# Splitting the modulation-weight loads of an AdaLN block over three DMA-issuing engines

## The chip, the cores and the metric

One Trainium2 chip, all 8 of its cores. Each core runs the same program on its own share of the tokens, with no exchange between cores. The metric is the device time of the slowest core in microseconds (us).

## The reference

One AdaLN transformer block on x of 4 x 4096 x 1024 in f32: six modulation vectors from a small condition c, attention between two layer norms, and a feed-forward layer whose operands are quantized to FP4 in blocks of 16. Cut to what the change touches and what uses it:

```python
mod = (silu(c) @ wmod).reshape(4, 6, 1, 1024)          # c: 4 x 1024, wmod: 1024 x 6144, f32
sa, ca, ga, sb, cb, gb = (mod[:, i] for i in range(6))
ga = (2 * (ga >= 0) - 1) * maximum(abs(ga), 0.25)      # gb likewise
h = layernorm(x) * (1 + ca) + sa
x = x + ga * attention(h, w_qkv, w_proj, b_proj)       # 16 heads
h = layernorm(x) * (1 + cb) + sb
x = x + gb * ffn_fp4(h, w_gate, w_up, w_down)          # 1024 -> 2816 -> 1024
```

## The kernel before

Two cores share one of the four sequences. A core owns 2048 tokens (its queries and its output) and computes keys and values for all 4096. x is kept channel-major, as `x_own`, 128 partitions x 8 x 2048 in f32 (8 MB). The program is a row of stages, each closed by `barrier()`, at which every engine waits for all semaphores: p0 (the modulation vectors), p1 (layer norm and the projections to q and k in slices of 512 tokens), pv (v), p3 (attention, with the quantization of the weights beside it on VectorE), p35 and p4 (softmax sums and output projection), p5 (second layer norm and quantization), p6 (feed-forward).

The change lies in p0. There the order on each engine is the order in which the code calls `em`, `dma` and `wt`:

- SP issues four loads at once: `ident32`, `ccol` (the condition), `bpcol` (a bias) and `x_own` in one transfer of 8 MB.
- ScalarE waits for `ccol` and `bpcol` and computes `silu_c` (L253).
- `wmod`, 1024 x 6144 f32, comes in KC = 8 chunks of 128 rows, 3 MB each, into two buffers `wmod_buf[kc % 2]`. All eight are issued by GpSimd (POOL). From the third on, GpSimd first waits until TensorE has finished the chunk that was in the buffer (`wm_done`).
- TensorE waits for the chunk (`t_wm`), for kc = 0 also for `silu_c`, and runs 48 matmuls on it, each of them a 128 x 128 block of `wmod` as stationary operand against one column of `silu_c` (L263). All 8 x 48 = 384 products add up in `mod_ps`. (The profile counts two instructions for each of these f32 matmuls, 768 in all.)
- VectorE copies `mod_ps` to `modc` (L272), makes `ca1`, `cb1`, `gacol` and `gbcol` from it, and the barrier follows. Then SP issues the loads of `xo` and GpSimd those of `wqk`, and p1 begins.

A DMA is issued through `_q_issue`. Each issuing engine has four semaphores that it takes in turn, and it waits for the transfer four places earlier in its own list before it issues the next:

```python
            s = QSEMS[q][QIDX[q]]
            QIDX[q] = (QIDX[q] + 1) % NQSEM
            wt(q, s, s.v)
            em(q, fn, s, 16)
```

Transfers issued by GpSimd run in the profile's queue q0 (software_dynamic), those issued by SP in q1 (hardware_dynamic). ScalarE issues none in the kernel before.

Of the kernel before, what the change touches and what calls it, by code (L numbers as in the profile page):

```python
# [14 lines left out]
P = 128  # L15
# [3 lines left out]
def build(cfg):  # L19
    N, D, NH, FI, SL = cfg["N"], cfg["D"], cfg["NH"], cfg["FI"], cfg["SL"]  # L20
# [24 lines left out]
    wmod_in = nc.dram_tensor("wmod", [D, 6 * D], F32, kind="ExternalInput").ap()  # L45
# [23 lines left out]
    def sb(name, shape, dt, stack=None):  # L69
        return (stack or es).enter_context(nc.sbuf_tensor(name, shape, dt))  # L70

    def psum(name, parts, free, dt=F32, stack=None):
        esz = 4 if dt == F32 else 2
        banks = -(-free * esz // 2048)
        return (stack or es).enter_context(
            nc.psum_tensor(name, [parts, banks * 2048 // esz], dt))
# [9 lines left out]
    mP, mV, mA = Sem("mP"), Sem("mV"), Sem("mA")  # L86
# [21 lines left out]
    with nc.Block("mk") as blk:  # L108
# [3 lines left out]
        def em(eng, fn, inc=None, k=1):  # L112
            if inc is None:
                E[eng](fn)
                return None
            inc.v += k
            E[eng](lambda e, fn=fn, h=inc.h, k=k: fn(e).then_inc(h, k))
            return inc.v

        def _q_issue(q, fn):  # L120
# [4 lines that stand above are left out]
            return (s, s.v)  # L125

        def dma(q, dst, src):
            return _q_issue(q, lambda e, dst=dst, src=src: e.dma_start(dst, src))
# [4 lines left out]
        def wtt(eng, tok):  # L133
            if tok:
                wt(eng, tok[0], tok[1])
# [5 lines left out]
        def wt(eng, sem, v=None):  # L141
            v = sem.v if v is None else v
            E[eng](lambda e, h=sem.h, v=v: e.wait_ge(h, v))

        def dr(eng):
            E[eng](lambda e: e.drain())  # L146

        def barrier():
            for eng in ("sync", "gpsimd", "scalar", "vector", "tensor"):
                for s in ALL_SEMS:  # L150
                    wt(eng, s)

        def act_table(set_id):
            E["scalar"](lambda e, i=set_id: e.add_instruction(  # L154
                mybir.InstLoadActFuncSet(
                    name=nc.get_next_instruction_name(),
                    act_func_set_id=i, ins=[], outs=[])))
# [76 lines left out]
        with contextlib.ExitStack() as p0:  # L234
            silu_c = sb("silu_c", [P, KC], F32, p0)
            wmod_buf = [sb(f"wmod{i}", [P, 6 * D], F32, p0) for i in range(2)]
            mod_ps = psum("mod_ps", P, 6 * KC, F32, p0)

            act_table(18)
            em("vector", lambda e: e.memset(ones128[:], 1.0))  # L240
            em("vector", lambda e: e.memset(ones1x[:], 1.0))
            em("vector", lambda e: e.memset(eps5[:], 1e-5), mV)
            em("vector", lambda e: e.memset(eps30[:], 1e-30), mV)
            t_id = dma("sync", ident32[:], ident_in[:])
            t_cc = dma("sync", ccol[:], cvec_in[:])
            t_bp = dma("sync", bpcol[:], bproj_in[:])
            dma("sync", x_own[:], xr[:, :, 0:T])
            wtt("vector", t_id)
            em("vector", lambda e: e.tensor_copy(identbf[:], ident32[:]), mV)
            dr("vector")  # L250
            wtt("scalar", t_cc)
            wtt("scalar", t_bp)
            v_silu = em("scalar", lambda e: e.activation(silu_c[:], ccol[:], AF.Silu), mA)  # L253
            wm_done = [0, 0]
            for kc in range(KC):
                if kc >= 2:
                    wt("gpsimd", mP, wm_done[kc % 2])
                t_wm = dma("gpsimd", wmod_buf[kc % 2][:], wmod_in[P * kc:P * (kc + 1), :])
                wtt("tensor", t_wm)
                if kc == 0:  # L260
                    wt("tensor", mA, v_silu)
                for m in range(6 * KC):
                    em("tensor", lambda e, kc=kc, m=m: e.matmul(  # L263
                        mod_ps[:, m:m + 1],
                        wmod_buf[kc % 2][:, P * m:P * (m + 1)],
                        silu_c[:, kc:kc + 1],
                        start=(kc == 0 and m == 0),
                        stop=(kc == KC - 1 and m == 6 * KC - 1)),
                        mP if m == 6 * KC - 1 else None)
                wm_done[kc % 2] = mP.v  # L270
            wt("vector", mP, mP.v)
            em("vector", lambda e: e.tensor_copy(modc[:], mod_ps[:, 0:6 * KC]), mV)  # L272
            dr("vector")
            cam = modc[:, 1 * KC:2 * KC]
            gam = modc[:, 2 * KC:3 * KC]
            cbm = modc[:, 4 * KC:5 * KC]
            gbm = modc[:, 5 * KC:6 * KC]
            em("vector", lambda e: e.tensor_scalar(ca1[:], cam, 1.0, None, ALU.add))
            em("vector", lambda e: e.tensor_scalar(cb1[:], cbm, 1.0, None, ALU.add))
            dr("vector")  # L280
            for g_src, g_dst in ((gam, gacol), (gbm, gbcol)):
                em("vector", lambda e, s=g_src, d=g_dst: e.scalar_tensor_tensor(
                    d[:], s, -1.0, s, ALU.mult, ALU.max))
                em("vector", lambda e, s=g_src: e.tensor_scalar(
                    smallf[:, 0:KC], s, 0.0, 2.0, ALU.is_ge, ALU.mult))
                dr("vector")
                em("vector", lambda e: e.tensor_scalar(
                    smallf[:, 0:KC], smallf[:, 0:KC], -1.0, None, ALU.add))
                em("vector", lambda e, d=g_dst: e.tensor_scalar(
                    d[:], d[:], 0.25, None, ALU.max))  # L290
                dr("vector")
                em("vector", lambda e, d=g_dst: e.tensor_tensor(
                    d[:], d[:], smallf[:, 0:KC], ALU.mult), mV)
                dr("vector")
            barrier()
# [822 lines left out]
def _get_nc():  # L1118
    if "nc" not in _NC_CACHE:
        _NC_CACHE["nc"] = build(CFG)  # L1120
    return _NC_CACHE["nc"]
# [44 lines left out]
if __name__ == "__main__":  # L1166
    nc = build(CFG)
    n = sum(1 for _ in nc.all_instructions())
    print("built OK; instructions:", n)
```

How the kernel before makes its waits and increments, by code:

```python
        def em(eng, fn, inc=None, k=1):  # L112
            if inc is None:
                E[eng](fn)
                return None
            inc.v += k
            E[eng](lambda e, fn=fn, h=inc.h, k=k: fn(e).then_inc(h, k))
            return inc.v
# [22 lines left out]
        def wt(eng, sem, v=None):  # L141
            v = sem.v if v is None else v
            E[eng](lambda e, h=sem.h, v=v: e.wait_ge(h, v))
```

## Time and profile before

| | us |
|---|---|
| median of the two timed runs (4413.93 and 4420.41) | 4417.17 |
| the profiled execution, device time | 4420.6 |
| its span on the slowest core, core 0 | 4419.1 |
| spans of the eight cores | 4396.6 to 4419.1 |
| TensorE busy (matmul) | 2298.0 |
| VectorE busy | 2800.1 |
| ScalarE busy | 1193.3 |
| GpSimd busy | 201.9 |

The profile is of core 0. Its span counts from the first to the last instruction, and the device time of that execution is 1.5 us more. Shares over the whole span mix eight stages, so for a change in one stage the time of that stage is to be looked at: p0 is the first 184 us or so, 4% of the span.

### The profile page before, as it was taken

What the parts mean: (1) busy time and instruction counts of PE and PEld (TensorE: products, weight loads), DVE (VectorE), ACT (ScalarE), POOL (GpSimd) and SP (SyncE); (2) the same over time, 40 slices, a digit from 0 to 9 for tenths busy, and PEclk for the clock granted to TensorE, in tenths of its full rate; (3) what the DMA queues carried; (4) which work ended last, traced back from release to release, by engine and by line L of the source; (5) the groups of instructions that cost most, each with busy time, mean ns of one, the idle gap of its engine ahead of it and who ended that gap; (6) DMA issues with size and microseconds to landing.
All of it is one profiled execution on the core that took longest, in us unless ns stands there. A gap on an engine that the chain in (4) does not pass through costs nothing.

```text
span 4419.1 us, 32886 instructions; the slowest of 8 cores (4396.6 to 4419.1 us)
## 1 busy us (share of the span) xinstructions
PE 2298.0 (52%) x9132; PEld 858.5 (19%) x9132; DVE 2800.1 (63%) x4084; ACT 1193.3 (27%) x1236; POOL 201.9 (5%) x324
## 2 busy tenths in 40 slices
PE   8656654978787878756555600022222164222227
PEld 8612211422222222211100200001111121111113
DVE  0066665329999999999712569966666724666661
ACT  0011111088898989866500000000000000000000
POOL 0001100000111010010000000000000000000000
PEclk9987877989999989977755755556666577666658
DMA  7511112312222222232310010011111012111102
GB/s 248 124 45 36 49 60 92 72 40 57 72 72 72 53 71 69 61 78 58 85 39 15 25 37 14 14 29 29 29 29 29 20 49 69 29 29 29 29 24 86
DMA packets 260929, 239.47 MB, mean 54 GB/s; under 512 B 193040, under 2 KB 229264, under 8 KB 256656
## 3 DMA queue, kind: packets, MB, share of 16 engines
q1 hardware_dynamic: 233360, 122.27, 10.9%
q0 software_dynamic: 27392, 115.11, 8.8%
q8 instruction: 79, 1.29, 0.1%
q14 instruction: 98, 0.80, 0.1%
HBM read 157.36 MB, written 46.66 MB: 46 GB/s over the span
## 4 chain that ended last, share of the span: by engine, by line
DVE 42%; PE 21%; DVEq 14%; DMA 10%; issue 5%; ACT 5%; SPq 3%; POOL 0%; ACTq 0%; POOLq 0%
DVEq L232 7%; DVEq L222 4%; PE dp_ps L1085 4%; ACT pb L738 3%; PE mod_ps L263 3%; PE bc L802 3%; PE v_ps L582 2%; SPq L131 2%; DVEq L146 2%; DMA wu_sb<-wuts 2%; PE g_ps L1034 2%; PE u_ps L1044 2%; DVE x_own L211 2%; DVE x_own L213 2%; DVE x_own L209 2%
## 5 line engine op out<-in xcount | busy, mean ns | idle before, releaser
L738 ACT ACTIVATE pb<-s_ps,negc 128x1024 bf16<-128x1024 f32 x1024 | 1037.0, 1233 | 118.3 <-PE s_ps L710 117.6
L1034 PE MATMUL g_ps<-wg_sb,h2q 128*128 128x512 bf16 (+1 forms) x768 | 189.4, 406 | 1282.0 <-DMA wu_sb<-wuts 1233.2
L706 PE MATMUL s_ps<-qb,kb 64*128 64x512 bf16 x1024 | 394.2, 388 | 183.3 <-ACT pb L738 116.3
L721 PE MATMUL pv_ps<-pb,vres 128*65 128x512 bf16 x992 | 414.5, 418 | 87.4 <-DVE O L772 87.4
L710 PE MATMUL s_ps<-qb,kb 64*128 64x512 bf16 x1024 | 407.1, 400 | 0.0
L1052 ACT ACTIVATE silu_sb<-g_ps 128x1024 bf16<-128x1024 f32 (+1 forms) x56 | 47.1, 840 | 1280.3 <-PE u_ps L1044 1280.3
L727 PE MATMUL pv_ps<-pb,vres 128*65 128x512 bf16 x992 | 389.6, 393 | 0.0
L1034 PEld LDWEIGHTS g_ps<-wg_sb,h2q 128*128 128x128 bf16 x768 | 81.9, 108 | 1383.3 <-issue 1317.3
L1057 DVE TENSOR_TENSOR hmul<-silu_sb,u_ps 128x1024 bf16<-128x1024 bf16 (+1 forms) x56 | 55.6, 992 | 430.6 <-ACT silu_sb L1052 356.2
L154 ACT ACT_TABLE_LOAD x5 | 6.4, 1283 | 933.6 <-DVE x_own L849 311.4
L464 PE MATMUL qk_ps<-h,wqk 128*128 128x512 bf16 x768 | 211.5, 426 | 34.5 <-ACT qkst L476 19.6
L706 PEld LDWEIGHTS s_ps<-qb,kb 64*128 64x128 bf16 x1024 | 94.0, 93 | 656.4 <-issue 656.4
L1085 PE MATMUL dp_ps<-hq,wd 128*128 128x512 bf16 x704 | 162.1, 395 | 73.6 <-DMA wd<-wdts 59.4
L802 PE MATMUL bc<-lnsums,ones1x 1*64 1x512 f32 x128 | 123.8, 1068 | 137.4 <-DMA lnsums<-lnsums 91.9
L263 PE MATMUL mod_ps<-silu_c,wmod 128*128 128x1 f32 x768 | 164.1, 352 | 16.6 <-ACT silu_c L253 16.0
L721 PEld LDWEIGHTS pv_ps<-pb,vres 128*65 128x65 bf16 x992 | 108.4, 109 | 325.7 <-issue 325.7
L263 PEld LDWEIGHTS mod_ps<-silu_c,wmod 128*128 128x128 f32 x768 | 164.0, 333 | 16.6 <-issue 16.6
L1044 PE MATMUL u_ps<-wu_sb,h2q 128*128 128x512 bf16 (+1 forms) x768 | 166.5, 370 | 0.0
L807 DVE TENSOR_TENSOR O<-O,bc 64x512 bf16<-64x512 bf16 x64 | 43.9, 685 | 186.6 <-PE bc L802 186.6
L476 ACT CAST qkst<-qk_ps 128x512 bf16<-128x512 f32 x96 | 56.2, 585 | 345.8 <-DVE qkn L440 306.4
L1097 DVE SCALAR_TENSOR_TENSOR x_own<-dp_ps,gbcol,x_own 128x512 f32<-128x512 f32 x32 | 24.0, 750 | 176.5 <-PE dp_ps L1085 173.5
L440 DVE TENSOR_REDUCE qkn<-nrm_ps 1x1 f32<-1x512 f32 x192 | 122.0, 671 | 12.3 <-PE nrm_ps L430 10.7
(170 smaller groups left out, 3824.2 us busy)
## 6 DMA issues: line engine op xcount, KB each, us to landing
wmod<-wmod POOLq DMA_DIRECT2D x8, 3072.0 KB, 13.2
x_own<-x SPq DMA_DIRECT2D x2, 8192.0 KB, 44.7
x_own<-wgate POOLq DMA_DIRECT2D x22, 512.0 KB, 4.6
x_own<-wup POOLq DMA_DIRECT2D x22, 512.0 KB, 4.6
x_own<-wdown POOLq DMA_DIRECT2D x16, 704.0 KB, 5.9
wd<-wdts SPq DMA_DIRECT2D x88, 128.0 KB, 2.1
wg_sb<-wgts SPq DMA_DIRECT2D x10, 1024.0 KB, 5.6
wu_sb<-wuts SPq DMA_DIRECT2D x10, 1024.0 KB, 8.0
```

The source lines that it names most:

```text
L232: V(lambda e: e.drain())
L263: em("tensor", lambda e, kc=kc, m=m: e.matmul(mod_ps[:, m:m + 1], wmod_buf[kc % 2][:, P * m:P * (m + 1)], silu_c[:, kc:kc + 1], start=(kc ...
L464: em("tensor", lambda e, oc=oc, kc=kc, pb=pb, bi=bi: e.matmul(qk_ps[pb][:, 0:SL], wqk_sb[kc][:, P * oc:P * (oc + 1)], h_buf[bi][:, kc, :], ...
L706: em("tensor", lambda e, kt=kt, qoff=qoff, pb=pb, sAB=sAB: e.matmul(sAB[:, 0:512], kbuf[pb][0:64, P * kt:P * (kt + 1)], qbuf[pb][0:64, qof ...
L710: em("tensor", lambda e, kt=kt, qoff=qoff, pb=pb, sAB=sAB: e.matmul(sAB[:, 512:1024], kbuf[pb][64:128, P * kt:P * (kt + 1)], qbuf[pb][64:1 ...
L721: em("tensor", lambda e, ktp=ktp, qs2p=qs2p, gp=gp, h0=h0: e.matmul(pv_ps[0][:, 512 * qs2p:512 * (qs2p + 1)], vres[:, ktp, 65 * h0:65 * (h ...
L727: lambda e, ktp=ktp, qs2p=qs2p, gp=gp, h1=h1: e.matmul(pv_ps[1][:, 512 * qs2p:512 * (qs2p + 1)], vres[:, ktp, 65 * h1:65 * (h1 + 1)], pbuf ...
L738: exp_at[g] = em("scalar", lambda e, sAB=sAB, pAB=pAB: e.activation(pAB[:, 0:1024], sAB[:, 0:1024], AF.Exp, bias=negc[:], scale=0.125), mA)
L802: p_bc = em("tensor", lambda e, qs=qs, b_=b_: e.matmul(bc_ps[b_:b_ + 64, 0:512], ones1x[:, 0:64], lnsums[0:1, QS * qs:QS * (qs + 1)], star ...
L1034: em("tensor", lambda e, kc=kc, qt=qt, iw=iw, tb=tb, tbase=tbase, off=off: e.matmul(g_ps[tb][:, off:off + iw], h2q[:, kc, tbase + P * qt:t ...
L1044: p_gu = em("tensor", lambda e, kc=kc, qt=qt, iw=iw, tb=tb, tbase=tbase, off=off: e.matmul(u_ps[tb][:, off:off + iw], h2q[:, kc, tbase + P ...
L1085: lambda e, ic=ic, ib=ib, j=j, qs=qs: e.matmul(dp_ps[2 * j + qs][:, 0:512], wd_sb[ib][:, P * j:P * (j + 1)], hq[:, ic, 512 * qs:512 * (qs ...
```

## The change

Every 3 MB chunk of `wmod` is loaded by two transfers of 1.5 MB, columns 0 to 3071 and columns 3072 to 6143. The two are issued by two different engines, which are taken in turn from the list GpSimd, SP, ScalarE: chunk kc has its left half from engine kc mod 3 and its right half from engine (kc + 1) mod 3. Both engines wait for the buffer from kc = 2 on, and TensorE waits for both halves before its 48 matmuls. Nothing else is edited.

| chunk | left half | right half |
|---|---|---|
| 0, 3, 6 | GpSimd | SP |
| 1, 4, 7 | SP | ScalarE |
| 2, 5 | ScalarE | GpSimd |

```diff
             wm_done = [0, 0]
+            wm_qs = ["gpsimd", "sync", "scalar"]
             for kc in range(KC):
                 if kc >= 2:
-                    wt("gpsimd", mP, wm_done[kc % 2])
-                t_wm = dma("gpsimd", wmod_buf[kc % 2][:], wmod_in[P * kc:P * (kc + 1), :])
+                    wt(wm_qs[kc % 3], mP, wm_done[kc % 2])
+                    wt(wm_qs[(kc + 1) % 3], mP, wm_done[kc % 2])
+                t_w1 = dma(wm_qs[kc % 3], wmod_buf[kc % 2][:, 0:3 * D],
+                           wmod_in[P * kc:P * (kc + 1), 0:3 * D])
+                t_wm = dma(wm_qs[(kc + 1) % 3], wmod_buf[kc % 2][:, 3 * D:6 * D],
+                           wmod_in[P * kc:P * (kc + 1), 3 * D:6 * D])
+                wtt("tensor", t_w1)
                 wtt("tensor", t_wm)
```

On SP, in p0, the new loads stand behind that of `x_own` (`d_sync0` to `d_sync3` are SP's four semaphores, `mP` is TensorE's; `wmod0` and `wmod1` are the two buffers):

```order
 L128 DMA x_own<-x 128x8x2048
+L143 UNCONDITIONAL_BRANCH
+L117 UNCONDITIONAL_BRANCH [waits d_sync0]
+L128 DMA wmod0<-wmod 128x3072
+L143 UNCONDITIONAL_BRANCH
+L117 UNCONDITIONAL_BRANCH [waits d_sync1]
+L128 DMA wmod1<-wmod 128x3072
+L143 UNCONDITIONAL_BRANCH
+L143 UNCONDITIONAL_BRANCH [waits mP]
+L117 UNCONDITIONAL_BRANCH [waits d_sync2]
+L128 DMA wmod1<-wmod 128x3072
```

The right half of chunk 0 is thus SP's fifth transfer and the left half of chunk 1 its sixth, and neither waits for a matmul.

On ScalarE, in p0, the first load stands behind the activation that makes `silu_c`:

```order
 L253 ACTIVATE silu_c<-ccol 128x8
+L143 UNCONDITIONAL_BRANCH
+L117 UNCONDITIONAL_BRANCH [waits d_scalar0]
+L128 DMA wmod1<-wmod 128x3072
+L143 UNCONDITIONAL_BRANCH
+L143 UNCONDITIONAL_BRANCH [waits mP]
+L117 UNCONDITIONAL_BRANCH [waits d_scalar1]
+L128 DMA wmod0<-wmod 128x3072
```

ScalarE now issues five transfers in this stage, where it issued none, and the first of them is the right half of chunk 1.

On GpSimd, in p0, five transfers of half a chunk stand where eight of a whole one stood. The first rows of the kernel before:

```order
L117 UNCONDITIONAL_BRANCH [waits d_gpsimd0]
L128 DMA wmod0<-wmod 128x6144
L143 UNCONDITIONAL_BRANCH
L117 UNCONDITIONAL_BRANCH [waits d_gpsimd1]
L128 DMA wmod1<-wmod 128x6144
```

and of the kernel with the change:

```order
L117 UNCONDITIONAL_BRANCH [waits d_gpsimd0]
L128 DMA wmod0<-wmod 128x3072
L143 UNCONDITIONAL_BRANCH
L143 UNCONDITIONAL_BRANCH [waits mP]
L117 UNCONDITIONAL_BRANCH [waits d_gpsimd1]
L128 DMA wmod0<-wmod 128x3072
```

GpSimd's second transfer now waits for a matmul: it is the right half of chunk 2.

## Rows read from the trace of the kernel before

**Rows 1.** The timeline of p0: start us, us, engine line op, idle before

```profile
2.56 0.39 SPq L128 DMA_DIRECT2D x_own<-x  x1
...
15.65 0.21 ACT L253 ACTIVATE silu_c<-ccol 128x8 f32<-128x8 f32 x1 [13.31 <-DMA bpcol<-bproj]
...
16.00 41.09 PE L263 MATMUL mod_ps<-silu_c,wmod 128*128 128x1 f32 x192 [16.00 <-ACT silu_c L253]
37.23 0.53 POOL L128 DMA_DIRECT2D wmod<-wmod  x1 [34.35 <-PE mod_ps L263]
...
57.67 123.01 PE L263 MATMUL mod_ps<-silu_c,wmod 128*128 128x1 f32 x576 [0.57 <-DMA wmod<-wmod]
57.72 0.53 POOL L128 DMA_DIRECT2D wmod<-wmod  x1 [19.95 <-PE mod_ps L263]
...
180.79 0.21 DVE L272 COPY modc<-mod_ps 128x48 f32<-128x48 f32 x1 [177.52 <-PE mod_ps L263]
...
183.91 1.00 SPq L128 DMA_DIRECT2D xo<-x  x2
```

**Rows 2.** Landing times of wmod's eight loads; then of its first two alone

```profile
DMA to landing us min/median/max: 12.0/13.2/26.1
...
DMA to landing us min/median/max: 13.7/19.9/26.1
```

**Rows 3.** DMA issues of the whole page: KB each, median us to landing

```profile
x_own<-x SPq DMA_DIRECT2D x2, 8192.0 KB, 44.7
...
wg_sb<-wgts SPq DMA_DIRECT2D x10, 1024.0 KB, 5.6
wu_sb<-wuts SPq DMA_DIRECT2D x10, 1024.0 KB, 8.0
```

**Rows 4.** DMA issues of the first 190 us, the same columns

```profile
x_own<-x SPq DMA_DIRECT2D x1, 8192.0 KB, 58.3
xo<-x SPq DMA_DIRECT2D x2, 2048.0 KB, 31.4
...
ident<-ident SPq DMA_DIRECT2D x1, 64.0 KB, 1.8
...
bpcol<-bproj SPq DMA_DIRECT2D x1, 4.0 KB, 13.5
```

**Rows 5.** DMA of the first 15 us: packets and queues

```profile
DMA packets 588, 3.59 MB, mean 239 GB/s; under 512 B 317, under 2 KB 445, under 8 KB 445
...
q0 software_dynamic: 158, 3.51, 79.2%
q1 hardware_dynamic: 430, 0.07, 2.5%
```

**Rows 6.** Stretches: us, busy of PE, PEld, DVE, ACT, POOL, PEclk, DMA share, GB/s

```profile
0.00:8.00 8.00, 0.00 (x0) 0.00 (x0) 0.46 (x5) 1.28 (x1) 1.42 (x6) 1.00 0.70 190
0.00:14.00 14.00, 0.00 (x0) 0.00 (x0) 0.46 (x5) 1.28 (x1) 1.42 (x6) 1.00 0.81 233
...
28.00:37.00 9.00, 9.00 (x44) 9.00 (x43) 0.00 (x0) 0.00 (x0) 0.00 (x0) 1.00 1.00 343
37.00:57.00 20.00, 20.00 (x95) 20.00 (x94) 0.00 (x0) 0.00 (x0) 0.53 (x1) 1.00 1.01 333
```

**Rows 7.** DMA moved in the first 39 us, then in the first 44 us

```profile
DMA packets 1363, 11.64 MB, mean 298 GB/s; under 512 B 336, under 2 KB 464, under 8 KB 464
...
DMA packets 1503, 13.15 MB, mean 299 GB/s; under 512 B 336, under 2 KB 464, under 8 KB 464
```

**Rows 8.** Landing times of the loads of xo in the first barrier's wake

```profile
DMA to landing us min/median/max: 20.5/31.4/42.2
```

**Rows 9.** Spans and clocks of the cores

```profile
core 0: 4419.1 us, clock 0.753
...
core 3: 4396.6 us, clock 0.752
```

## The prediction

> **What bounds the kernel now.** The change touches only the first stage, so I read the timeline of that stage first, to see what each matmul of the modulation product waited for. TensorE starts at 16.00 us and runs to 57.09 (192 instructions), waits 0.57 us, and runs from 57.67 to 180.68 (576 instructions) [rows 1]. That is 768 instructions in 164.1 us, 0.2137 us each, 20.5 us for a chunk of 96, in one row without a gap but for those 0.57 us. The granted clock is 1.00 in all stretches of it, the upper level, also before TensorE had begun [rows 6]. So from 16 us on the stage is bound by TensorE, and the loads are hidden under it: a chunk of 3 MB lands 12.0 to 26.1 us after its issue, 13.2 in the middle [rows 2], and has a chunk's 20.5 us for it.
>
> What decides the start is the second thing to see. TensorE waited for `silu_c`, that for `bpcol` [rows 1], which took 13.5 us to land while `ident`, issued 1 us earlier in the same queue, took 1.8 [rows 4]. The view of the queues shows why: in the first 15 us the software queue moved 3.51 MB, which is chunk 0 and a little of chunk 1, and the hardware queue 0.07 MB, the three small loads [rows 5]. `x_own` had moved nothing. It was issued at 2.56 and landed 58.3 us later, at 60.9 [rows 1, 4], and nobody in this stage wants it. Chunk 0, issued ahead of it at 1.67 us, landed 13.7 us later, at 15.4 [rows 2]. The kernel before thus has its order of urgency right, because the urgent data are in another queue than the bulky ones.
>
> The DMA engines themselves are full: 343 GB/s in 28 to 37 us, where only `x_own` was under way, and 333 in 37 to 57, where chunk 2 was beside it [rows 6]. A second queue adds no bandwidth.
>
> **The change part by part.** *The matmuls.* The same 768, in the same order, 164.1 us. No gain from loads that are faster, since only 0.57 us of waiting for a load is there.
>
> *The right half of chunk 0.* This is the term that counts. It is issued by SP right behind `x_own`, without any wait. Are transfers of one hardware queue served one after the other or side by side? The trace has two pairs issued back to back on SP. `wg_sb` and `wu_sb`, 1 MB each, land after 5.6 and 8.0 us [rows 3]; at 343 GB/s 1.05 MB takes 3.1 us, so the second lands one such time behind the first, less the half microsecond by which it was issued later. The two `xo` loads land after 20.5 and 42.2 us [rows 8], the second twice as late. Both pairs look like one after the other; side by side the two of a pair would land together. So chunk 0 is whole only when `x_own` is through. Sizes: the left half of chunk 0, 1.57 MB; `x_own`, 8.39; the right half of chunk 0, 1.57; the small loads, 0.07. That is 11.6 MB. ScalarE issues the right half of chunk 1 (1.57 MB) once `silu_c` is done, near 10 us, in a queue of its own. Is that ahead of the end or behind it? The trace has no transfer issued by ScalarE. Ahead of it, the sum is 13.2 MB, behind it 11.6. In the kernel before the later software transfer got its share beside `x_own` (chunk 2 landed within 20 us in the middle of it [rows 1]), so I take 13.2.
>
> When has this core moved so much? The trace of before says so directly, as the DMA engines were full there too from about 3 us on: 11.64 MB by 39 us and 13.15 MB by 44.0 [rows 7]. So 13.2 MB by 44.1. From the last byte to the release of the waiting engine add 1.5 us: chunk 0 (3.15 MB) was through at about 14 us (233 GB/s x 14 us = 3.26 MB [rows 6]) and landed at 15.4. TensorE starts at 45.6 us where it started at 16.0: 29.6 us later. With 11.6 MB it is 39 + 1.5 = 40.5, 24.5 us later, the lower bound if the queue is in order. For the upper one I take the slowest rate of a large transfer in that queue: two loads of `x_own` have the median 44.7, the first took 58.3, so the reload in the middle of the kernel took 31.1 us [rows 3, 4], 270 GB/s. The left half is through at 8 us (190 GB/s x 8 = 1.52 MB [rows 6]), the other 11.6 MB take 43.0: start at 51.0, 35 us later.
>
> The Trainium skill (page DMA: Bandwidth & Descriptors, section Queues, rings and completion order) says that SP and ScalarE each own one ring on each of the same 16 DMA engines, that descriptors of a ring are taken in order, and that an engine goes round between the rings that have work. By that rule the ScalarE half gets its turns beside `x_own`, and the sum is 13.2 MB. No row here shows the ScalarE ring.
>
> *`silu_c`.* With only 1.57 MB ahead of it in the software queue, `bpcol` should land near 8 us and not at 15.6. That is worth 7 us only if chunk 0 were there, and it isn't. Nothing gained.
>
> *Chunk 1.* Its left half is the next in SP's queue, 1.57 MB behind chunk 0: 4.6 us at 343 GB/s, landing at about 50. Chunk 0's matmuls last until 45.6 + 20.5 = 66.1, so it is covered by 16 us.
>
> *Chunks 2 to 7.* Both halves are issued when the buffer is free, and have 20.5 us. At that time nothing else is under way, unlike in the kernel before, where chunk 2 had `x_own` beside it: issued at 37.23, landed at 57.67, the 0.57 us of waiting [rows 1]. That wait goes: -0.6. The 16 transfers of half a size in place of 8 cost issue time on SP, ScalarE and GpSimd (about 0.5 us each [rows 1]), which do nothing else in this stage. In the four-place rotation the transfer waited for is always one of earlier chunks or, for the left half of chunk 4 on SP, `x_own`, long landed by then. If that cover were gone, each late chunk would cost its excess over 20.5 us; that is a rival below.
>
> *The rest.* VectorE's small work and the barrier (180.68 to 183.9) move as they are. The loads of `xo` and `wqk` are issued after the barrier with all slots free, as before. `x_own` lands at about 42 us in place of 60.9, which is of use to nobody before 184. Later stages have the same instructions.
>
> Sum: +29.6 - 0.6 = +29.0 us, with bounds +24 and +34. The profiled execution took 4420.6, 3.4 us above the median of the runs shown (4417.2). So a profiled run like it would be 4450, and against the median I predict 4446 us, 0.7% slower. A comparison of this kernel can tell about 2% (88 us) from no change, so this is "within 2%".
>
> The same page of the Trainium skill (section Rules for kernel authors) says that spreading DMAs over SP, ACT and GpSimd for bandwidth doesn't help, as all run on the same 16 engines. The trace agrees: 333 GB/s with both queues, 343 with one [rows 6]. A gain from the split alone would be 0 by the rule and 0.57 us by the row.
>
> **The rivals.** *Transfers of one queue run side by side.* Then the right half of chunk 0 doesn't wait for all of `x_own`. If it comes with the left one, chunk 0 is whole at 15.4 as before and TensorE starts there: -0.6 - 0.6, 4416. If four transfers share 343 GB/s evenly from 8 us on (`x_own`, this half, two of chunk 1), it takes 6.28 MB, 18 us, and with 1.5 us TensorE starts at 27.8: +11, 4428. In the best case the start follows the earlier `silu_c`, at about 8.5: 4409. For it: `ident` and `ccol` landed quickly though more was issued behind them, which proves little. Against it: both pairs of rows 3 and 8. Chance 0.09.
>
> *The hardware queue carries less than in the stretch I read.* In my sum the rate before 28 us is partly the software queue's. At 270 GB/s it gives +34.4: 4452. For it: the reload's 31.1 us. Against it: 343 GB/s at 28 to 37 us in that same queue. Chance 0.09.
>
> *Slower by much: the later chunks become late.* Two halves on two queues, one of them served after the other, and TensorE waits for the later one. The place is the wait at the head of each chunk, the price seven times the excess over 20.5 us. If every chunk took 26.1 us, as the slowest did [rows 2], it would be 7 x 5.6 = 39, in all +68: 4485. At the 42.2 us of the slowest `xo` load it would be 7 x 21.7 = 152, in all +181: 4598. It passes 2% from 20.5 + (88 - 29) / 7 = 28.9 us a chunk. Against it: both of those rows had 5 MB or more beside them; 3.15 MB at 333 GB/s takes 9.4 us and the latency 1.5. Chance 0.03, of which 0.02 above 2%.
>
> **How the numbers follow.** The in-order case (forecast) has 0.79, the three rivals 0.09, 0.09 and 0.03. The range goes from 4428 (the even sharing) to 4462: the upper bound 4452 and 10 us for what one execution differs from another, as the cores of one run already lie 4396.6 to 4419.1 apart [rows 9]; about 0.15 lies outside. Faster by over 2% needs 88 us out of a stage with 0.57 us of waiting for loads and 16 us of start: 0.01. Slower by over 2% is the third rival's part: 0.02. Within 2%: 0.97.
>
> **What would show it.** Right: no matmul of the first product before 40 us, released by a `wmod` load; `silu_c` done near 9 us; `x_own` landing near 42 us, the right half of chunk 0 some 5 us later; then 164 us of matmuls without a gap; `xo` issued at about 213 us and not 183.9; the later stages as long as before. Wrong: TensorE starting before 30 us (side by side), a wait before chunk 2 or later (late chunks), or a difference that arises after the first barrier.

## The result and the profile after

The changed kernel took 4470.35 us (median of 23 runs, 4445.48 to 4509.45), the kernel before 4420.0 (median of 22 runs, 4412.63 to 4461.3). The ratio is 1.0092, with a 95% interval of 1.0063 to 1.012; it and the medians differ because it leaves out runs in which a die had a clearly lower clock, and as the profiled run of the changed kernel has a little of that on its second die (0.731 against 0.752), I read it on core 0, which has the clock of before. The interval is 28 to 53 us, 41 in the middle: slower by less than the 2% that count as a difference. The forecast was +29 us, 4446, within 4428 to 4462; 1.0092 x 4417.2 is 4458.

The timeline of the first stage on core 0 of the changed kernel (start us, us, what, idle before) answers to [rows 1]:

```profile
1.68 0.69 POOL L128 DMA_DIRECT2D wmod<-wmod  x1 [0.98 <-POOLq L38]
2.10 0.38 SPq L128 DMA_DIRECT2D bpcol<-bproj  x1
2.56 0.39 SPq L128 DMA_DIRECT2D x_own<-x  x1
3.06 170.57 SPq L128 DMA_DIRECT2D wmod<-wmod  x6
...
12.57 0.21 ACT L253 ACTIVATE silu_c<-ccol 128x8 f32<-128x8 f32 x1 [10.22 <-DMA bpcol<-bproj]
12.64 161.03 ACTq L128 DMA_DIRECT2D wmod<-wmod  x5
...
50.16 163.97 PE L269 MATMUL mod_ps<-silu_c,wmod 128*128 128x1 f32 x768 [50.16 <-DMA wmod<-wmod]
71.43 0.54 POOL L128 DMA_DIRECT2D wmod<-wmod  x1 [69.07 <-PE mod_ps L269]
...
214.24 0.21 DVE L278 COPY modc<-mod_ps 128x48 f32<-128x48 f32 x1 [210.91 <-PE mod_ps L269]
...
217.36 1.00 SPq L128 DMA_DIRECT2D xo<-x  x2
```

TensorE starts at 50.16 us where it started at 16.00, and what released it is no longer `silu_c` (done at 12.8) but a load of `wmod`. Then all 768 instructions run in one row of 163.97 us: the 0.57 us of before is gone. The loads of `xo`, the first thing behind the barrier, are issued at 217.36 in place of 183.91, 33.5 us later; over the eight cores this shift is 33.5 to 36.9 us. The lowest runs of the two kernels stand as far apart, 32.9 us (4445.48 and 4412.63). Of the two profiled executions, the whole spans of cores 1 to 3 differ by about as much (29.5, 35.5 and 32.7 us), that of core 0 by only 17.7: behind the first stage core 0 of the kernel before took 15.8 us longer than core 0 of the changed one, cores 1 to 3 between 1.6 us less and 5.4 us more. So the loss is read from the first stage, not from core 0's span.

The DMA issues of the first 50 us on the same core (KB each, us to landing) show the order in SP's ring:

```profile
x_own<-x SPq DMA_DIRECT2D x1, 8192.0 KB, 43.7
wmod<-wmod SPq DMA_DIRECT2D x2, 1536.0 KB, 47.6
wmod<-wmod POOLq DMA_DIRECT2D x1, 1536.0 KB, 10.6
wmod<-wmod ACTq DMA_DIRECT2D x1, 1536.0 KB, 14.8
```

`x_own` lands at 2.56 + 43.7 = 46.3 us. The 47.6 is the median of SP's two halves, 46.9 and 48.3. The half of chunk 0 behind `x_own` lands at 3.06 + 46.9 = 50.0, when its sibling from GpSimd has been there since 12.3. ScalarE's half of chunk 1, issued at 12.64, is there at 27.4: it got its turns beside `x_own`. The Trainium skill (DMA: Bandwidth & Descriptors, section Queues, rings and completion order) says that SP and ScalarE own one ring each on every DMA engine and that the engine goes round between them; the 14.8 us of that row agree, and the queue view now lists ScalarE's transfers by themselves, as q10.

### The profile page after: what moved, and what is told of

Its sections match the earlier page's. It is cut to its first block, busy times and chain, and to the rows that moved or that the text cites. A ratio compares the mean times of both kernels' runs of the same rounds, so it can differ in the third digit from the quotient of the medians.

```text
span 4468.3 us, 32837 instructions; the slowest of 8 cores (4429.3 to 4468.3 us)
## 1 busy us (share of the span) xinstructions
PE 2338.9 (52%) x9053; PEld 865.6 (19%) x9132; DVE 2801.4 (63%) x4084; ACT 1195.8 (27%) x1236; POOL 200.4 (4%) x321
## 3 DMA queue, kind: packets, MB, share of 16 engines
q10 hardware_dynamic: 720, 7.86, 0.6%
## 4 chain that ended last, share of the span: by engine, by line
DVE 39%; PE 22%; DVEq 13%; DMA 10%; ACT 7%; issue 6%; SPq 3%; POOL 0%; ACTq 0%; POOLq 0%
DVEq L232 7%; ACT pb L744 6%; PE dp_ps L1091 4%; PE mod_ps L269 4%; DVEq L222 4%; PE bc L808 3%; PE v_ps L588 2%; SPq L131 2%; PE g_ps L1040 2%; DVEq L146 2%; DMA wu_sb<-wuts 2%; PE u_ps L1050 2%; PE pj_ps L844 2%; DVE x_own L213 1%; DVE x_own L209 1%
## 5 line engine op out<-in xcount | busy, mean ns | idle before, releaser
L1040 PE MATMUL g_ps<-wg_sb,h2q 128*128 128x512 bf16 (+1 forms) x755 | 199.8, 425 | 1257.5 <-DMA wu_sb<-wuts 1209.5
L712 PE MATMUL s_ps<-qb,kb 64*128 64x512 bf16 x1024 | 405.6, 399 | 177.3 <-ACT pb L744 119.5
L727 PE MATMUL pv_ps<-pb,vres 128*65 128x512 bf16 x992 | 423.7, 427 | 86.7 <-DVE O L778 86.7
L716 PE MATMUL s_ps<-qb,kb 64*128 64x512 bf16 x1024 | 415.7, 409 | 0.0
L733 PE MATMUL pv_ps<-pb,vres 128*65 128x512 bf16 x992 | 399.3, 403 | 0.0
L1050 PE MATMUL u_ps<-wu_sb,h2q 128*128 128x512 bf16 (+1 forms) x756 | 176.7, 388 | 0.8
```

The costliest lines, as they stand in the source:

```text
L712: em("tensor", lambda e, kt=kt, qoff=qoff, pb=pb, sAB=sAB: e.matmul(sAB[:, 0:512], kbuf[pb][0:64, P * kt:P * (kt + 1)], qbuf[pb][0:64, qof ...
L716: em("tensor", lambda e, kt=kt, qoff=qoff, pb=pb, sAB=sAB: e.matmul(sAB[:, 512:1024], kbuf[pb][64:128, P * kt:P * (kt + 1)], qbuf[pb][64:1 ...
L727: em("tensor", lambda e, ktp=ktp, qs2p=qs2p, gp=gp, h0=h0: e.matmul(pv_ps[0][:, 512 * qs2p:512 * (qs2p + 1)], vres[:, ktp, 65 * h0:65 * (h ...
L733: lambda e, ktp=ktp, qs2p=qs2p, gp=gp, h1=h1: e.matmul(pv_ps[1][:, 512 * qs2p:512 * (qs2p + 1)], vres[:, ktp, 65 * h1:65 * (h1 + 1)], pbuf ...
L1040: em("tensor", lambda e, kc=kc, qt=qt, iw=iw, tb=tb, tbase=tbase, off=off: e.matmul(g_ps[tb][:, off:off + iw], h2q[:, kc, tbase + P * qt:t ...
L1050: p_gu = em("tensor", lambda e, kc=kc, qt=qt, iw=iw, tb=tb, tbase=tbase, off=off: e.matmul(u_ps[tb][:, off:off + iw], h2q[:, kc, tbase + P ...
```

## The experiments

The times of a stage are of core 0, from the timeline, unless other cores are named. Seven of the nine runs ask where the loss is, two try a faster version.

### The load of x_own behind the urgent ones

```diff
-            dma("sync", x_own[:], xr[:, :, 0:T])
             wtt("vector", t_id)
 ...
+                if kc == 1:
+                    dma("sync", x_own[:], xr[:, :, 0:T])
                 wtt("tensor", t_w1)
```

> The changed kernel, with the 8 MB load of x_own issued by SP behind its two first loads of wmod (the right half of chunk 0 and the left half of chunk 1) and not ahead of them. Theory (the right half of chunk 0 waits for x_own because it stands behind it in SP's ring): TensorE's first product starts at 14 to 18 us in place of 50.2, the loads of xo are issued at 180 to 185 us in place of 217.4, and the kernel takes about 34 us less than the changed one, that is the time of the kernel before within 5 us. Rival (the split over three engines is slow in itself, or the engines are simply full): the start stays above 30 us.

```profile
2.56 0.86 SPq L128 DMA_DIRECT2D wmod<-wmod  x2
3.50 0.67 SPq L128 DMA_DIRECT2D x_own<-x  x1
...
15.61 163.97 PE L270 MATMUL mod_ps<-silu_c,wmod 128*128 128x1 f32 x768 [15.61 <-DMA wmod<-wmod]
...
182.80 1.00 SPq L128 DMA_DIRECT2D xo<-x  x2
```

(the timeline of core 0). The start is at 15.61, on the eight cores 15.6 to 16.7, and `xo` is issued at 182.80: on core 0 the whole loss is gone, with the split and the three engines still there. On cores 6 and 7 chunk 2 comes 2.2 and 1.3 us late, and `xo` is issued at 185.3 and 184.8, 2.3 and 0.9 us later than in the kernel before. Against the kernel before the ratio is 1.0011 (0.9969 to 1.0053): no difference is seen, though the interval, from 14 us less to 23 more, is too wide to confirm the "within 5 us" by itself. `x_own` lands at 64.9 us, 18.6 later than in the changed kernel, and nobody minds. The loss was one line's place.

### The same bytes, another ring

```diff
-            dma("sync", x_own[:], xr[:, :, 0:T])
+            dma("scalar", x_own[:], xr[:, :, 0:T])
```

> The changed kernel, with the load of x_own issued by ScalarE, as its first transfer, in place of SP. As many bytes are under way as in the changed kernel, but now the right half of chunk 0 is first in SP's ring, and the right half of chunk 1 is behind x_own in ScalarE's. Theory (order inside a ring): TensorE's first product starts at 15 to 28 us; chunk 1 is whole only when x_own is through, near 50 us, so TensorE stands still between chunk 0 and chunk 1 for 2 to 15 us, and the loads of xo are issued at 215 to 220 us with almost the same loss as in the changed kernel. Rival (all transfers under way share the engines and what counts is their bytes, 13 MB, not the ring): the start is at 45 to 52 us and there is no gap behind chunk 0.

```profile
22.20 0.21 ACT L253 ACTIVATE silu_c<-ccol 128x8 f32<-128x8 f32 x1 [19.86 <-DMA bpcol<-bproj]
...
29.79 20.61 PE L269 MATMUL mod_ps<-silu_c,wmod 128*128 128x1 f32 x96 [29.79 <-DMA wmod<-wmod]
...
53.71 143.49 PE L269 MATMUL mod_ps<-silu_c,wmod 128*128 128x1 f32 x672 [3.31 <-DMA wmod<-wmod]
...
200.43 1.01 SPq L128 DMA_DIRECT2D xo<-x  x2
```

(the timeline of core 0). The same transfers are wanted and the same 13 MB or so are under way, but the start is at 29.8 and not at 50.2. That is 1.8 us above my range, and 15 below the rival's. So the order inside the ring is the larger part, while sharing the engines costs too: 29.8 is 14 us later than with `x_own` behind. Chunk 1, whose half now stands behind `x_own`, makes the gap of 3.31 us (2.3 to 6.5 on the eight cores). For the end I had written 215 to 220, which was wrong arithmetic: 53.71 + 143.5 + 3.2 is 200.4.

### Half of x_own ahead

```diff
-            dma("sync", x_own[:], xr[:, :, 0:T])
+            dma("sync", x_own[:, 0:KC // 2, :], xr[:, 0:KC // 2, 0:T])
 ...
+                if kc == 1:
+                    dma("sync", x_own[:, KC // 2:KC, :], xr[:, KC // 2:KC, 0:T])
```

> The changed kernel, with x_own loaded in two transfers of 4 MB, the first ahead of SP's two loads of wmod as now, the second behind them. The dose is halved. Theory (the start is the time at which the bytes ahead in the ring are through): 4.2 MB less at 290 to 320 GB/s, 13 to 14.5 us, so the start is at 36 to 37.5 us in place of 50.2 and the loads of xo are issued at 203 to 205 us. Rival (any x_own load ahead costs the same, for instance by its issue): 50 us. Rival (the ring isn't the cause): below 20 us.

The start is at 34.37 us (34.1 to 35.9 on the eight cores), and `xo` is issued at 201.57. The dose works: nothing of `x_own` ahead gives 15.6, half of it 34.4, all of it 50.2, that is 18.8 us for the first 4.2 MB and 15.8 for the second. The start is 1.6 us below the range I gave, since 4.2 MB took 15.8 us off and not 14.5 at most: 266 GB/s, less than the 290 I had as the slowest. The rate here is 327 GB/s from 14 to 34 us; it is the changed kernel that has a slow stretch ahead of its start, 184 GB/s in 32 to 38 us, of which more below.

### Whole chunks, all on SP

```diff
-                    wt("gpsimd", mP, wm_done[kc % 2])
-                t_wm = dma("gpsimd", wmod_buf[kc % 2][:], wmod_in[P * kc:P * (kc + 1), :])
+                    wt("sync", mP, wm_done[kc % 2])
+                t_wm = dma("sync", wmod_buf[kc % 2][:], wmod_in[P * kc:P * (kc + 1), :])
```

> The kernel before, with the eight whole chunks of wmod issued by SP, behind x_own, in place of GpSimd: no split, and one engine. Theory (the loss is what stands ahead in the ring): 11.6 MB are ahead of chunk 0's end, TensorE starts at 40 to 46 us, and the loads of xo are issued at 207 to 213 us, a loss of 24 to 29 us. Rival (the split in halves or the three engines cost it): no loss, the start at 16 us.

```profile
4.73 0.21 ACT L253 ACTIVATE silu_c<-ccol 128x8 f32<-128x8 f32 x1 [2.38 <-DMA bpcol<-bproj]
45.58 163.97 PE L263 MATMUL mod_ps<-silu_c,wmod 128*128 128x1 f32 x768 [45.58 <-DMA wmod<-wmod]
...
212.77 1.00 SPq L128 DMA_DIRECT2D xo<-x  x2
```

(the timeline of core 0). The kernel before, with no split and no second engine for `wmod`, loses 28.9 us by having them issued on SP behind `x_own`. The start is at 43.8 to 50.3 on the eight cores, above my 46 on four of them, and the loss is 27.4 to 34.0. `silu_c` is ready at 4.9 us, the earliest of all kernels, and it is of no use.

### The split alone

```diff
-            wm_qs = ["gpsimd", "sync", "scalar"]
+            wm_qs = ["gpsimd"] * 3
```

> The changed kernel with both halves of every chunk issued by GpSimd: the split alone, without the other two engines. Theory (the split costs nothing, only the place behind x_own does): TensorE's first product starts at 15 to 17 us, 164 us of products without a gap of over 1.5 us, and the loads of xo are issued at 182 to 186 us, as in the kernel before. Rival (twice as many transfers cost by themselves): over 190 us.

```profile
11.80 0.21 ACT L253 ACTIVATE silu_c<-ccol 128x8 f32<-128x8 f32 x1 [9.45 <-DMA bpcol<-bproj]
...
19.44 41.09 PE L269 MATMUL mod_ps<-silu_c,wmod 128*128 128x1 f32 x192 [19.44 <-DMA wmod<-wmod]
...
64.62 123.01 PE L269 MATMUL mod_ps<-silu_c,wmod 128*128 128x1 f32 x576 [4.10 <-DMA wmod<-wmod]
...
190.86 1.00 SPq L128 DMA_DIRECT2D xo<-x  x2
```

(the timeline of core 0). A miss: the split isn't free when GpSimd issues both halves. `bpcol` lands 3.9 us earlier than in the kernel before (`silu_c` starts at 11.8, where it was 15.65 [rows 1]), TensorE starts 3.4 us later, released by chunk 0, and chunk 2 makes a gap of 4.10 us where it made 0.57. `xo` is issued 7.0 us later. The queues of the first 15 us (packets, MB, share of 16 engines) show where the time went; in the kernel before they had 158 and 3.51, and 430 and 0.07 [rows 5]:

```profile
q0 software_dynamic: 236, 2.70, 65.5%
q1 hardware_dynamic: 515, 0.75, 16.1%
```

A packet of the software queue is half as large as before (11 KB on average in place of 22), and `x_own`, which stands behind `bpcol` in SP's ring, has moved 0.7 MB by 15 us where it had moved nothing. These are bytes that chunk 0 lacks. So the trace shows that `x_own` gets its turns earlier and that chunk 0 pays; that the size of the packets is the reason was not tested by itself. The changed kernel's late start is not this effect: its left half of chunk 0 is there at 12.3 us, 38 us ahead of the right one.

### Another order of the three engines

```diff
-            wm_qs = ["gpsimd", "sync", "scalar"]
+            wm_qs = ["gpsimd", "scalar", "sync"]
```

> The changed kernel with the three engines taken in the order GpSimd, ScalarE, SP, so that SP's first load of wmod is the right half of chunk 1, and chunk 0 has GpSimd and ScalarE. Theory (only what stands behind x_own in SP's ring is late, and a later chunk has one chunk's time of slack for it): chunk 0's right half is issued at 12 to 13 us behind silu_c and lands some 15 us later, so the first product starts at 25 to 30 us; chunk 1 is whole at 48 to 52 us, a gap of 0 to 5 us; the loads of xo are issued at 194 to 199 us, about 20 us ahead of the changed kernel's 217.4. Rival (three rings in use are slow whatever the order): 210 us or more.

The first product starts at 27.09 us, then there is a gap of 8.88 us before chunk 1, and `xo` is issued at 203.28. So the start is as expected, and the gap and the end are longer than I gave: SP's half of chunk 1 is there at 56.6, not at 48 to 52. On cores 3 to 7 the products end 3.6 to 7.0 us later still, and on core 5 `xo` is issued at 210.3, where the rival's range began; what speaks against the rival is the start at 25.9 to 28.1 on all cores. The direction holds: a half behind `x_own` that is wanted one chunk later has 20.5 us of slack, and the loss is 19 us on core 0 in place of 33.5 (19 to 27 on the eight cores in place of 33.5 to 36.9). Merely swapping two names in the list gives 14 us back on core 0, 8 to 16 over the cores.

### Nothing behind chunk 0

```diff
+                if kc == 1:
+                    wtt("sync", t_wm)
+                    wtt("scalar", t_wm)
                 if kc >= 2:
```

> The changed kernel, with both loads of chunk 1 issued only when chunk 0's right half has landed. So nothing stands behind it in SP's ring and ScalarE issues nothing beside it: 11.6 MB are all that is under way. In the changed kernel the start was at 50.2 us on core 0, 4.6 us behind the 45.6 of my sum. Theory A (the 16 engines don't keep pace, so that part of what stands behind in the ring, and ScalarE's 1.57 MB, are moved before chunk 0 is whole): the start is at 40 to 43 us, as my lower bound for 11.6 MB had it (40.5). Theory B (SP's ring, with x_own alone in it, runs slower than the mixed traffic of the kernel before that I took the curve from): the start is at 44 to 47 us. In both, chunk 1 is whole some 10 to 12 us later, inside chunk 0's 20.5 us of products, without a gap.

The stretches of core 0 (us, busy of PE, PEld, DVE, ACT, POOL, PEclk, DMA share, GB/s), then what had been moved by 40 and by 44 us:

```profile
14.00:28.00 14.00, 0.00 (x0) 0.00 (x0) 0.00 (x0) 0.00 (x0) 0.00 (x0) 1.00 1.00 339
28.00:32.00 4.00, 0.00 (x0) 0.00 (x0) 0.00 (x0) 0.00 (x0) 0.00 (x0) 1.00 1.13 166
...
28.00:36.00 8.00, 0.00 (x0) 0.00 (x0) 0.00 (x0) 0.00 (x0) 0.00 (x0) 1.00 1.02 240
36.00:44.00 8.00, 0.00 (x0) 0.00 (x0) 0.00 (x0) 0.00 (x0) 0.00 (x0) 1.00 0.51 214
```

```profile
DMA packets 1715, 11.22 MB, mean 280 GB/s; under 512 B 339, under 2 KB 467, under 8 KB 467
...
DMA packets 1760, 11.61 MB, mean 264 GB/s; under 512 B 352, under 2 KB 480, under 8 KB 480
```

The start is at 44.28 us (44.1 to 48.4 on the eight cores): theory B's range but for the slowest core, and not for its reason. Of the 11.61 MB only 0.4 were left at 40 us, and they took 4 us more with the engines busy for 0.51 of 36 to 44 us. So the 16 engines don't finish together, and the transfer is whole when the last has finished. The rate is the other part, but SP's ring with `x_own` alone in it isn't slow as such: it moves 339 GB/s from 14 to 28 us, as much as the kernel before. What is missing is missing in 28 to 32 us, 166 GB/s with the engines busy all the time, and the other seven cores fall as well, each to between 119 and 201 GB/s for at least 2 us between 28 and 32 us.

### A version that is faster than both

In the kernel before TensorE stands from the first barrier to 225 us for the loads of `wqk`, though the statistics of the first slice need only `x_own`, which is there. The wait is put where `wqk` is first used. The rows of the kernel before (core 0; the profile puts this wait down to `xo`, on core 6 to `wqk`):

```profile
225.17 0.58 PE L356 MATMUL st_ps<-xbch,ones 128*1 128x512 bf16 x1 [44.49 <-DMA xo<-x]
...
257.10 3.15 PE L464 MATMUL qk_ps<-h,wqk 128*128 128x512 bf16 x7 [13.88 <-DVE h L409]
```

And the edit:

```diff
-            for tok in wqk_toks:
-                wtt("tensor", tok)
 ...
             v_h_cur = emit_h(0)
+            for tok in wqk_toks:
+                wtt("tensor", tok)
```

> The kernel before, with TensorE's wait for the loads of wqk moved from the head of the second stage to behind the statistics and the broadcast of the first slice, which need x_own alone. In the kernel before, TensorE stands from 184 to 225 us for them, and the first projection starts at 257.1. Theory (the same kind of loss as in the change, work that waits for bytes it doesn't need): the first projection starts when wqk is there, at 225 to 230 us, and the kernel takes 25 to 32 us less than before. Rival (the time comes back later, because the next slice or the GpSimd queue is the bound there): the first projection starts earlier, but the end of the second stage moves by less than 10 us.

```profile
198.46 2.04 PE L387 MATMUL bc_ps<-rs_row,ones1x 1*128 1x512 f32 x2 [5.44 <-DVE nmr_row L378]
...
224.09 7.16 PE L462 MATMUL qk_ps<-h,wqk 128*128 128x512 bf16 x23 [21.89 <-DMA hscr<-h]
```

(the timeline of core 0; the releaser named there is `hscr`, but on the other seven cores the same wait is put down to `wqk`, and it is the one that was moved). The first projection starts at 224.1 in place of 257.1, and the copy that closes the second stage is at 713.2 in place of 745.9: 32.7 us are kept on core 0, 20.9 to 34.4 on the eight cores. The kernel takes 0.9939 of the time before (0.9905 to 0.9974), 27 us less.

With the loads of `xo` held back as well (the run above with this edit):

```diff
                     if s >= OSL + 2:
                         wt("sync", mP, pe_done[s - 2])
+                    else:
+                        wt("sync", mP, pe_done[s - 4])
```

> As e6_wqk_wait_late, and the two loads of xo (4 MB, wanted by the fifth and sixth slice only, near 490 us) are issued by SP only when the first and the second slice are through, in place of beside the loads of wqk. Theory (they take bandwidth from wqk): wqk is complete at 210 to 218 us, the first projection starts at 216 to 221 us, 5 to 10 us ahead of e6, and the kernel takes 30 to 42 us less than before. Rival (wqk's loads, which convert f32 to bf16 and go through GpSimd's queue, are bound by that queue and not by the engines' bandwidth): the first projection starts as in e6, within 2 us.

```profile
202.10 0.53 POOL L128 DMA_DIRECT2D wqk<-wqkv  x1 [3.35 <-DMA wqk<-wqkv]
...
218.64 6.94 PE L464 MATMUL qk_ps<-h,wqk 128*128 128x512 bf16 x23 [14.27 <-DVE h L409]
```

(the timeline of core 0). The last load of `wqk` is issued at 202.1, where it was 207.8 in the run above, and the first projection waits for VectorE's `h` and no longer for a load: 5.5 us earlier (7 to 11 on the other cores), so the queue of GpSimd wasn't the bound. But the closing copy is at 712.6, only 0.6 us earlier (from 5.5 earlier to 2.7 later on the eight cores). Most of it is given back within the second stage. The ratio is 0.9922 (0.9888 to 0.9956), 34 us less than before, and the two intervals overlap, so nothing can be said of the difference between these two versions. Both intervals lie below 1, and that of the changed kernel lies above it: both versions are faster than either, by less than the 2% that count as a difference against the kernel before.

## Why the prediction was right

The direction, the place and the mechanism were right, step by step:

- *TensorE bounds the stage from its start on, loads gain nothing.* Shown: 163.97 us in the changed kernel and in every variant whose loads leave no gap, and 0.57 us was all there was to gain.
- *The right half of chunk 0 waits for `x_own` in SP's ring.* Shown three ways: with `x_own` behind, the loss is 0 on core 0 and 2.3 us at most; with half of it ahead, the loss is 18 us; with another ring for it, the start comes 20 us earlier with the same bytes. The rival of transfers side by side in one ring is out.
- *The later chunks aren't late.* Shown by the row of 768 without a gap; the rival that needed 28.9 us a chunk is out.
- *`silu_c` gains nothing.* Right in effect. It started at 12.57 and not near 8 us: 1.33 of the 1.57 MB ahead of `bpcol` had been moved by 8 us, but `bpcol` landed only with the end of that transfer, at 12.5, where the half landed at 12.3.

What was mis-sized is the main term, "TensorE starts at 45.6 us": it was 50.2 on core 0 and up to 52.8 on others, so that +29.6 was +34.2, near the upper bound of 35 (which left out its own 1.5 us from the last byte to the release; with them it would be 36.5). Two parts of that term failed. "13.15 MB by 44.0" was read from core 0 of the kernel before; the changed kernel had less by then, and by the start it had moved more than my 13.2 (core 0, first 44 and first 50 us):

```profile
DMA packets 1817, 12.37 MB, mean 281 GB/s; under 512 B 349, under 2 KB 477, under 8 KB 477
...
DMA packets 2000, 14.31 MB, mean 286 GB/s; under 512 B 372, under 2 KB 500, under 8 KB 500
```

0.8 MB less at 44 us is 2.5 us at its 323 GB/s. The other 2 us are in the 1.5 "from the last byte to the release". These leave out that the engines finish at different times: 1.1 MB of what stood behind chunk 0 had been moved before chunk 0 was whole, 3.5 us in place of 1.5. With nothing behind it this became an idle tail, 0.4 MB in 4 us.

The stretches of the changed kernel's core 0 show when the 0.8 MB went missing (us, busy of PE, PEld, DVE, ACT, POOL, PEclk, DMA share, GB/s):

```profile
14.00:28.00 14.00, 0.00 (x0) 0.00 (x0) 0.00 (x0) 0.00 (x0) 0.00 (x0) 1.00 1.02 327
...
32.00:38.00 6.00, 0.00 (x0) 0.00 (x0) 0.00 (x0) 0.00 (x0) 0.00 (x0) 1.00 0.98 184
38.00:44.00 6.00, 0.00 (x0) 0.00 (x0) 0.00 (x0) 0.00 (x0) 0.00 (x0) 1.00 1.03 369
```

By 28 us it had moved 7.77 MB and the kernel before 7.86; the deficit is made in 32 to 38 us alone, and all eight cores have it there (160 to 225 GB/s). The same thing is in other runs at other times: in 28 to 32 us with nothing behind chunk 0, between 18 and 30 us with whole chunks on SP (every core falls to between 111 and 242 GB/s for 2 us), and in the kernel before itself, on cores 1, 2, 5 and 7 in 36 to 38 us (160 to 233) and on core 0 at 56 to 58 us (193). Core 0, from which my sum was read, had no such stretch before 44 us; that was chance, and the forecast came out low by it. So the rival of a slower hardware queue, at 0.09 and +34, had the right size and the wrong reason: outside that stretch SP's ring carried as much as the queues of the kernel before. What makes the rate fall for some us, with the engines busy all the time, stays open.

Against the interval of +28 to +53 us for the whole kernel the stage accounts for 33.5 to 36.9. The 4 to 7 us up to the middle of the interval aren't explained, and the interval doesn't require them. That the measured 4458 lies in the stated range owes something to its margin: the sum's own upper bound was 4452, and the 10 us for scatter brought the range to 4462.

## What to carry to other kernels

Before a transfer is put on another engine's queue, look at what stands ahead of it there: behind a bulky load an urgent one waited here for every byte of it, and free issue slots tell nothing of that. Spreading loads over engines added no bandwidth here (327 GB/s in 14 to 28 us with the change, 328 before); what counts is the order of urgency within each ring, and a load that nobody wants soon goes last. The same reading, "who waits here for bytes that it doesn't need yet", found 27 to 34 us in the next stage.

## What the runs showed of the hardware that was not expected

- A transfer of 4 KB (`bpcol`, 128 rows of 32 bytes), third in SP's ring behind two small ones, took until 4.7 us to release ScalarE when the other rings were empty (whole chunks on SP), until 11.7 to 15.6 us beside GpSimd's load, and until 22.2 us with `x_own` issued first on ScalarE's ring. So the work in other rings delays it although nothing large stands ahead of it in its own.
- Issuing the same 3 MB as two transfers of 1.5 MB from GpSimd made chunk 0 whole at 19.4 in place of 15.4 us, against a large load in the hardware queue, which had moved 0.7 MB by 15 us where it had moved nothing.
- Engines that share one transfer don't end together: 3% of 11.61 MB took 4 of its 44 us.
- On all eight cores together the rate falls for some us while the engines stay busy: 160 to 225 GB/s in 32 to 38 us of the changed kernel, between 327 in 14 to 28 and 369 in 38 to 44 us (core 0). It comes at another time in another kernel, and no run shows why.
